# Local attention's softmax in two halves of four heads, one-column routing operations with scalar operands, and a new order of the second stage

## The reference, cut to what matters

```python
def local_attn(x, Wqkv, Wout):            # 8 heads of 64, windows of 64 rows
    q, k, v = map(towin, split(x @ Wqkv.T, 3))
    ke, ve = (expand(k), expand(v))       # window before, own, after: 192 keys
    sim = einsum('bhnid,bhnjd->bhnij', q, ke) * SCALE
    sim = where(valid, sim, -1e9)
    attn = softmax(sim, axis=-1)
    return (attn @ ve) @ Wout.T

def route(x, routing_token, num_tokens):  # for queries 256, for keys 512 of 2048 rows
    s = x @ routing_token
    for _ in range(50):
        a = logk - logsumexp(s + bb)
        bb = -relu(s + a)
    return top_k(exp(s + a + bb), num_tokens)

light = local_attn(_ln(x), Wqkv, Wout_l)
heavy = heavy_attn(x[rows chosen], x[rows chosen], ...)
out = null_q everywhere, heavy where chosen; x + out + light
```

## Time and profile before

| what | value |
|---|---|
| median of 3 runs | 3353.71 us (3351.18 to 3353.83) |
| profiled execution | 3355.9 us, its span 3354.0 us, mean granted clock 0.978 |
| PE busy | 3137.5 us, 94% of the span |
| DVE busy | 2644.0 us, 79% |
| ACT, POOL busy | 1535.5 us, 46%; 1608.7 us, 48% |
| stage 2, DVE, one instruction: sadd, olo, yadd, vadd, xlo | 1216, 689, 683, 676, 678 ns |
| stage 2, DVE: reciprocal of den; routing's na | 203, 266 ns |
| stage 2, ACT: pcopy, softexp, ohi | 588, 1918, 582 ns |
| scores of four heads on PE (8 matmuls); pv of a tile (32) | 1.13 us; 1.97 us |
| weights for stage 3, three DMAs | 2048, 1024 and 1024 KB, landing 9.8, 12.2 and 15.4 us after issue |
| store of y, load of XY, load of XL | 256 KB each, landing 3.6, 3.4 and 3.6 us after issue |

### The profile page before, as it was taken

One profiled execution on the slowest core, in us unless ns is written; L12 is line 12 of the kernel. 1 busy time (PEld: TensorE's weight loads), 2 busy tenths in 40 slices (PEclk: granted clock), 3 DMA queues, 4 the chain that ended last, 5 costly groups with the idle time before them and its releaser, 6 DMA issues.

```text
span 3354.0 us, 52534 instructions
## 1 busy us (share of the span) xinstructions
PE 3137.5 (94%) x20930; PEld 2439.9 (73%) x20930; DVE 2644.0 (79%) x4310; ACT 1535.5 (46%) x2509; POOL 1608.7 (48%) x1043
## 2 busy tenths in 40 slices
PE   7999999999999999999979999998999999968998
PEld 4777777777777777777757777776777777756786
DVE  4788888988999999999947788778877885556453
ACT  1566665656665555545533333332233333324343
POOL 1656555555555665656613444443444444464200
PEclk9999999999999999999989999999999999989999
DMA  4001111010102111110120111111122221132100
GB/s 153 30 28 51 41 38 51 28 57 26 69 26 94 51 41 44 50 48 23 64 79 17 51 51 66 52 51 35 64 80 85 70 85 51 51 117 70 32 14 13
DMA packets 87445, 180.05 MB, mean 54 GB/s; under 512 B 9526, under 2 KB 10294, under 8 KB 85664
## 3 DMA queue, kind: packets, MB, share of 16 engines
q1 hardware_dynamic: 82512, 161.73, 14.0%
q0 software_dynamic: 3968, 10.50, 1.0%
q10 hardware_dynamic: 720, 4.46, 0.3%
HBM read 106.05 MB, written 70.60 MB: 53 GB/s over the span
## 4 chain that ended last, share of the span: by engine, by line
PE 67%; DVE 23%; issue 6%; ACT 2%; POOL 1%; DMA 1%; SPq 1%; POOLq 0%; DVEq 0%; ACTq 0%
PE ps L263 14%; PE ps L265 13%; PE ps L264 13%; PE ps L258 8%; PE ps L270 5%; PE ps L477 4%; PE ps L1125 3%; PE ps L1105 2%; PE ps L486 2%; DVE mx L639 2%; DVE Sb L633 2%; DVE rcol L1267 2%; PE ps L1699 2%; DVE sTa L677 1%; DVE dw L1228 1%
## 5 line engine op out<-in xcount | busy, mean ns | idle before, releaser
L823 POOL TENSOR_TENSOR Sb<-Sb,dn 128x1232 f32<-128x1232 f32 x128 | 294.8, 2303 | 276.8 <-DVE dn L647 276.8
L818 POOL TENSOR_TENSOR Sb<-Sb,mx 128x1232 f32<-128x1232 f32 x128 | 289.1, 2258 | 284.3 <-DVE mx L639 282.1
L1514 POOL TENSOR_TENSOR Sw<-Sw,dw 128x2048 f32<-128x2048 f32 x64 | 230.7, 3604 | 372.4 <-DVE dw L1231 372.4
L773 ACT COPY PT<-ps 77x512 f32<-77x512 f32 x512 | 292.1, 578 | 183.5 <-PE ps L477 182.5
L258 PE MATMUL ps<-KB,QT 128*128 128x308 f32 x1024 | 329.9, 431 | 43.2 <-DVE XB L659 26.8
L1509 POOL TENSOR_TENSOR Sw<-Sw,mw 128x2048 f32<-128x2048 f32 x64 | 232.3, 3629 | 231.4 <-DVE mw L1223 231.4
L1458 ACT COPY PU<-ps 128x512 f32<-128x512 f32 x256 | 139.5, 588 | 405.3 <-PE ps L270 405.3
L477 PE MATMUL ps<-ident,Sb 128*77 128x128 f32 x2048 | 295.2, 277 | 1.7 <-POOL Sb L823 1.3
L477 PEld LDWEIGHTS ps<-ident,Sb 128*77 128x77 f32 x2048 | 242.8, 147 | 71.0 <-issue 33.6
L633 DVE TENSOR_TENSOR Sb<-ps,dlt 128x308 f32<-128x308 f32 x512 | 233.1, 464 | 32.7 <-PE ps L258 30.7
L258 PEld LDWEIGHTS ps<-KB,QT 128*128 128x128 f32 x1024 | 169.0, 191 | 104.1 <-DVE XB L659 44.8
(11 more groups left out here) (275 smaller groups left out, 8148.1 us busy)
## 6 DMA issues: line engine op xcount, KB each, us to landing
XB<-in_x SPq DMA_DIRECT2D x16, 1024.0 KB, 5.3
x_scratch<-XB SPq DMA_DIRECT2D x16, 1024.0 KB, 4.3
XB<-x_scratch SPq DMA_DIRECT2D x16, 1024.0 KB, 5.7
x_scratch<-XB SPq DMA_DIRECT2D x64, 256.0 KB, 2.0
XL<-x_scratch SPq DMA_DIRECT2D x64, 256.0 KB, 3.6
XY<-x_scratch SPq DMA_DIRECT2D x64, 256.0 KB, 3.4
y_scratch<-XY SPq DMA_DIRECT2D x64, 256.0 KB, 3.6
out<-yo SPq DMA_DIRECT2D x64, 256.0 KB
```

Of the source, the lines that this page charges most:

```text
L773: A.copy(PT[:, 4 * g:4 * g + 4, :], ps[0:NK, bank("PT", n, g), :].rearrange("p (c n) -> p c n", c=4)).then_inc(a_pt, 1)
L818: G.tensor_tensor(sv, sv, last(mx[:, n % 2, :], NK), ALU.subtract).then_inc(g_sub, 1)
L823: G.tensor_tensor(sv, sv, last(dn[:, n % 2, :], NK), ALU.mult).then_inc(g_norm, 1)
L1514: G.tensor_tensor(sv, sv, last(dw[:, n % 2, :], 256), ALU.mult).then_inc(bg_norm, 1)
```

## The change

It has three parts. In the routing, three operations on single columns are written as one tensor with scalar operands (`tensor_scalar`) in place of two tensors (`tensor_tensor`, `scalar_tensor_tensor`): `M`, `T` and `dd`. In the local attention, `smax`, `sub`, `softexp`, `den` and `norm` become two instructions per tile, each for four heads (128x1024), with their semaphores counted twice per tile; `ptrans` waits for its own half. All four tables of stage 2 get new places.

```diff
--- before.py
+++ after.py
@@ -142,17 +142,18 @@
 
 
 
-TILE_B = {"loadxy": (18,), "scores": (-5, 20), "sadd": (5, 39), "smax": (56,), "sub": (136,), "softexp": (142,),
-        "den": (115,), "norm": (215,), "ptrans": (151, 156, 171, 174), "pcopy": (184, 186, 197, 205), "pv": (184,),
-        "ohi": (230,), "olo": (204,), "wo": (213,), "yadd": (229,), "yo": (477,), "storey": (270,)}
-BLOCK_B = {"loadxl": (-766, -741, -690, -490), "tail": (-269,), "ln": (-650, -619, -561, -306),
-        "turn": (-319, -317, -299, -296), "xhi": (-294, -289, -266, -260), "xlo": (-298, -297, -294, -293),
-        "qk": (-278, -261, -258, -232, -202, -163, -143, -126),
-        "qkcopy": (-248, -217, -171, -162, -131, -111, -97, -72), "edge": (-53,), "v": (-96, -58, 1, 50, 59),
-        "vadd": (-32, -23, 26, 75, 78)}
-GATHER = {"grows": (-228, -148, -102, -44, -39, 91), "gstats": (82,), "grs": (216,), "gnorm": (127,),
-        "gsq": (505,), "gpow": (679,), "gfin": (1443,)}
-ROUTE = {"rtp": 25, "rtv": 37, "rta": 60, "rts": -102}
+TILE_B = {"loadxy": (-232,), "scores": (-9, 36), "sadd": (15, 41), "smax": (20, 67), "sub": (257, 294),
+        "softexp": (89, 126), "den": (114, 117), "norm": (341, 349), "ptrans": (116, 122, 137, 144),
+        "pcopy": (141, 162, 174, 175), "pv": (183,), "ohi": (220,), "olo": (203,), "wo": (207,), "yadd": (241,),
+        "yo": (537,), "storey": (62,)}
+BLOCK_B = {"loadxl": (-990, -867, -797, -732), "tail": (-130,), "ln": (-600, -519, -517, -324),
+        "turn": (-336, -334, -302, -297), "xhi": (-296, -294, -269, -267), "xlo": (-300, -299, -293, -291),
+        "qk": (-291, -285, -250, -244, -206, -179, -161, -134),
+        "qkcopy": (-231, -221, -186, -181, -160, -134, -90, -81), "edge": (80,), "v": (-105, -46, 3, 46, 59),
+        "vadd": (-48, -20, 39, 73, 106)}
+GATHER = {"grows": (-98, -77, -20, 70, 190, 271), "gstats": (102,), "grs": (424,), "gnorm": (139,),
+        "gsq": (833,), "gpow": (580,), "gfin": (1915,)}
+ROUTE = {"rtp": 21, "rtv": 35, "rta": 55, "rts": -246}
 
 
 def order_b():
@@ -1040,6 +1041,10 @@
 
             return 16 * (e // 17) + min(e % 17, 15)
 
+        def weights(n, p):
+
+            return Sw[:, n % 2, 1024 * p:1024 * p + 1024].rearrange("p (h n) -> p h n", h=4)
+
         def values(i):
             return 5 if i % 4 == 3 else 4
 
@@ -1110,7 +1115,7 @@
 
             def ptrans(n, q):
                 p = take_b("PT", n, q)
-                pe.wait_ge(bg_norm, n + 1)
+                pe.wait_ge(bg_norm, 2 * n + q // 2 + 1)
                 turn4(p, Sw[:, n % 2, 512 * q:512 * q + 512]).then_inc(b_pt, 1)
 
             def pv(n, i):
@@ -1218,17 +1223,16 @@
                                 ps[:, b0:b0 + 2, :].rearrange("p b (k n) -> p (b k) n", k=2),
                                 mid(msk[:, which, :], 4), ALU.add).then_inc(bv_sadd, 1)
 
-            def wmax(n, i):
-                ve.wait_ge(bv_sadd, 2 * n + 2)
-                V.tensor_reduce(mw[:, n % 2, :], Sw[:, n % 2, :].rearrange("p (h n) -> p h n", h=8), X,
-                                ALU.max).then_inc(bv_max, 1)
-
-            def den(n, i):
-                ve.wait_ge(ba_exp, n + 1)
-                V.tensor_reduce(dw[:, n % 2, :], Sw[:, n % 2, :].rearrange("p (h n) -> p h n", h=8), X,
-                                ALU.add).then_inc(v_chain, vc.up())
+            def wmax(n, p):
+                ve.wait_ge(bv_sadd, 2 * n + p + 1)
+                V.tensor_reduce(mw[:, n % 2, 4 * p:4 * p + 4], weights(n, p), X, ALU.max).then_inc(bv_max, 1)
+
+            def den(n, p):
+                d = dw[:, n % 2, 4 * p:4 * p + 4]
+                ve.wait_ge(ba_exp, 2 * n + p + 1)
+                V.tensor_reduce(d, weights(n, p), X, ALU.add).then_inc(v_chain, vc.up())
                 ve.wait_ge(v_chain, vc.n)
-                V.reciprocal(dw[:, n % 2, :], dw[:, n % 2, :]).then_inc(bv_den, 1)
+                V.reciprocal(d, d).then_inc(bv_den, 1)
 
             def olo(n, i):
                 ve.wait_ge(ba_ohi, n + 1)
@@ -1264,7 +1268,7 @@
                     it, part_ = lse(k)
                     if part_ == 0:
                         new_na(it)
-                        V.tensor_tensor(M, smax, na, ALU.min).then_inc(v_chain, vc.up())
+                        V.tensor_scalar(M, smax, na, None, ALU.min).then_inc(v_chain, vc.up())
                         ve.wait_ge(v_chain, vc.n)
                         V.tensor_scalar(zr[:, :], sr[:, :], na, M, ALU.min, ALU.subtract).then_inc(bv_z, 1)
                 elif k == BITS - 2:
@@ -1283,7 +1287,7 @@
                         ve.wait_ge(b_rt, 3 + ITERS - 1 + q)
                         V.tensor_scalar(sel, ps[:, p, 0:1], kcol, None, ALU.is_ge).then_inc(bv_rt, 1)
                         ve.wait_ge(bv_rt, 3 + q)
-                        V.scalar_tensor_tensor(T, dd, sel, T, ALU.mult, ALU.add).then_inc(v_chain, vc.up())
+                        V.tensor_scalar(T, dd, sel, T, ALU.mult, ALU.add).then_inc(v_chain, vc.up())
                     else:
                         ve.wait_ge(ba_e, ITERS)
                     ve.wait_ge(v_chain, vc.n)
@@ -1291,7 +1295,7 @@
                         V.tensor_scalar(cand.bitcast(I32), T.bitcast(I32), 1 << (29 - q), None,
                                         ALU.bitwise_or).then_inc(v_chain, vc.up())
                         ve.wait_ge(v_chain, vc.n)
-                        V.tensor_tensor(dd, cand, T, ALU.subtract)
+                        V.tensor_scalar(dd, cand, T, None, ALU.subtract)
                         V.tensor_scalar(zr[:, :], sr[:, :], cand, 0.0, ALU.is_ge, ALU.add,
                                         accum_out=part).then_inc(bv_z, 1)
                     else:
@@ -1462,9 +1466,9 @@
                 ac.wait_ge(b_wo, n - 1)
                 A.copy(OT[0][:, n % 2, :, :], quad(bank_b("PV", n))).then_inc(ba_ohi, 1)
 
-            def softexp(n, i):
-                ac.wait_ge(bg_sub, n + 1)
-                A.activation(Sw[:, n % 2, :], Sw[:, n % 2, :], ACT.Exp).then_inc(ba_exp, 1)
+            def softexp(n, p):
+                ac.wait_ge(bg_sub, 2 * n + p + 1)
+                A.activation(weights(n, p), weights(n, p), ACT.Exp).then_inc(ba_exp, 1)
 
             def rt(k):
                 if LSE <= k < BITS - 2:
@@ -1503,15 +1507,15 @@
                 if i % 4 == 3:
                     G.memset(KU[:, s, :, 576:640], 0.0).then_inc(bg_edge, 1)
 
-            def sub(n, i):
-                sv = Sw[:, n % 2, :].rearrange("p (h n) -> p h n", h=8)
-                gp.wait_ge(bv_max, n + 1)
-                G.tensor_tensor(sv, sv, last(mw[:, n % 2, :], 256), ALU.subtract).then_inc(bg_sub, 1)
-
-            def norm(n, i):
-                sv = Sw[:, n % 2, :].rearrange("p (h n) -> p h n", h=8)
-                gp.wait_ge(bv_den, n + 1)
-                G.tensor_tensor(sv, sv, last(dw[:, n % 2, :], 256), ALU.mult).then_inc(bg_norm, 1)
+            def sub(n, p):
+                gp.wait_ge(bv_max, 2 * n + p + 1)
+                G.tensor_tensor(weights(n, p), weights(n, p), last(mw[:, n % 2, 4 * p:4 * p + 4], 256),
+                                ALU.subtract).then_inc(bg_sub, 1)
+
+            def norm(n, p):
+                gp.wait_ge(bv_den, 2 * n + p + 1)
+                G.tensor_tensor(weights(n, p), weights(n, p), last(dw[:, n % 2, 4 * p:4 * p + 4], 256),
+                                ALU.mult).then_inc(bg_norm, 1)
 
             def yo_(n, i):
                 gp.wait_ge(bv_y, n + 1)
```

## The result

The changed kernel takes 3261.43 us (median of 4 runs, 3259.53 to 3267.83) against 3353.77 for the kernel before beside it: ratio 0.973, interval 0.9713 to 0.9746, 92 us faster. The profiled execution has a span of 3257.7 us and a clock of 0.987. The forecast was 3299 with a range of 3268 to 3336. The direction was right, the gain was forecast 38 us too small, and the measured time lies outside the range.

The account below looks back on a forecast made before the run. The prediction took stage 2 to be bound by TensorE, with 90 us of holes behind late DVE steps. Gains of 22 (logsumexp rounds), 15 (bits), 3 (indices) and 15 (end), 55 us off 3353.7, gave 3299, range 3268 to 3336.

Parts of the forecast that it names:

- What bounds the kernel: Stage 2: TensorE is the busiest engine with 90 us of holes; only holes and clock lost behind them can be won.
- Rival 3: One-column scalar forms in the routing wait as well; halves leave 5 us and the end 12: 3337 us, chance 0.05.
- The wait moves there: Logsumexp rounds: the DVE row behind M, 345 to 1280 ns before, inherits the wait, now shorter and once less.
- What it buys is latency: Softmax halves: first four heads reach PE earlier, and a POOL instruction holds DVE at most 1.9 us.
- The clock: Behind each PE hole part of the work runs at 1.2 instead of 2.4 GHz, counted as 1.2 us per hole.
- (a): PE order: first-half ptrans moves directly behind wo(n-1); 2 us of slack, so it costs nothing.
- (b): DVE at a block's start: first xlo ends some 8 us after scores, PE needs it after 8.5, so holes close.
- (c): POOL order: yo(n-2) fills the exponential's time; sub(n,1) queues behind edge(i), about 5 us later, at no cost.
- (d): SP queue: loads and stores move up, SP stands still 3.6 us per store; DVE may wait for XL in the index stretch.
- (e): Stage 2's end: gather pairs move between POOL's sub halves; last tiles take 11.3 us each, the end gains 15 (5 to 20).
- Number 2: Rival where everything closes in stage 2: gain 29 + 21 + 12 + 20 = 82 us, 3272 us, chance 0.10.
- The signs: Profile marks: column forms under 300 ns, PE waits under 6 us, clock 0.99, no XY wait, stage 3 55 us earlier.

Follow-up runs that it names:

- e8: Kernel before with the three scalar-operand column operations and the softmax halves together, everything else in the old order; ratio 0.9776 to the kernel before.
- e4: Changed kernel with all four groups of a tile's weight transposes in one row on PE again; 3284.8 us, ratio 0.9791 to the kernel before.
- e1: Kernel before with only the three one-column operations in scalar-operand form; ratio 0.9863 to the kernel before.
- e3: Kernel before with only the softmax steps in halves, each second half directly behind the first, columns and order as before; ratio 0.9808.
- e6: Kernel before with only the changed kernel's order, each softmax step once at its second half's place, columns as before; ratio 1.0625.
- e7: Changed kernel with the DMA-issuing steps on SP (loadxy, storey, loadxl, index steps) back at their old places; ratio 0.9783 to the kernel before.
- e9: Changed kernel with a block's fourth layer norm row behind the first two xlo, and olo ahead of the routing step; ratio 0.9714 to the kernel before.

## Why the prediction was wrong, step by step

**The step that failed** is the price of PE's busy time in the sum. Windows from tile 0 to tile 56 of the kernel before, e8 and after (columns as in the earlier trace rows):

```profile
1764.47:2866.29 1101.82, 1045.41 (x6629) 822.96 (x6630) 871.41 (x1143) 375.02 (x647) 487.81 (x220) 0.98 0.18 58
```

```profile
1765.12:2803.97 1038.85, 1025.15 (x6629) 811.62 (x6630) 757.44 (x1308) 379.97 (x702) 505.48 (x331) 1.00 0.19 62
```

```profile
1763.01:2794.79 1031.78, 1015.84 (x6635) 813.41 (x6636) 760.82 (x1310) 385.42 (x703) 508.18 (x332) 1.00 0.19 64
```

The forecast took 40 us for these tiles (22, 15 and 3); 70.0 came. Of them 40.5 are holes that closed (56.4 to 15.9 us) and 29.6 are a shorter busy time for the same work. The forecast priced that busy time at 1.2 us for each of seven holes and 3.3 us in the bits, 11.7 us at most. It fell by 20.3 us with the old order already (e8), where the clock goes from 0.98 to 1.00, and by another 9.3 us through the new order, which the prediction set at nothing. The holes alone were near the forecast where it looked closely (13.9 us of the 20.3 counted in the rounds, 17.8 of 17.7 in the bits) and above it in the index stretch (6.5, where holes and clock together were put at 3) and from tile 48 to 56 (2.3 for nothing).

**What bounds the kernel** was right as far as it went: a PE stage with holes, DVE late behind POOL. The sentence "only holes and what the clock loses behind them can be won" failed. The 1.6 us of hole in 195 hid a row of transposes that costs 1.7 us a block in the old order and 2.1 in e4, 1.0 of the 1.7 while PE counts as busy.

**Part 1** was right in kind: under 300 ns, waiting for nobody, 200 to 276 ns. The Trainium skill's rule that `tensor_scalar` too can block ("SBUF — State Buffer", section "Who interferes with whom") isn't seen on one column, in the 109 instances of the three; on 128x128 it is (e1: mean 1748 ns). Rival 3 is out. "The wait moves there" was right for columns alone (85.6 us in e1) and wrong beside the halves: L1273 sums to 32.0 us, where before had 32.8.

**Part 2** was right in sizes (1.90 us, 128 times) and wrong in worth. "What it buys is latency" and a bound of 1.9 us on a wait missed that waiting falls by more than half; e3 alone is 64 us, where rival 3 left 5 to the halves outside the end. That is also where the index stretch's gain comes from (9.7 us with halves alone, 1.3 with columns alone). I had it at 3, between a loss on the queue and 12.

**The clock** is the mis-sized term. "I count 1.2 us for each hole" rests on too little: the transposes behind the hole alone give 0.8 (1.97 against 1.14, and the earlier trace rows), the rest was judgement, and the block shows 1.9 to 3.3 for a hole of 3.15 us (before against e8). In tiles 0 to 24 the clock's part is 12.4 us (448.8 to 436.4 us of busy time from before to e8) against the 8.4 counted. That moves my upper bound for the logsumexp rounds from 29 to 33, and the measured 29.7 lies inside. The rest of that term's miss is choice: I took 22 because the holes closed "with half a microsecond to spare". They closed but for 0.8 us a block, and those 0.8 cost no clock. In the bits PE's busy time falls by 4.9 us from before to e8 and by 6.0 to after (160.4 to 154.5, tiles 24 to 32), where I had 3.3.

**Part 3.** (a) "Cost nothing" for the split of `ptrans` missed its gain: the whole order gains 7.0 us on the old one from tile 0 to 56 (e8 against after), and without the split it loses 16.6 (e4). That PE does not wait for `norm` held (0.6 us in two waits from 1762 to 2882); e6 shows what the same order costs without halves. (b) held but for 0.8 us. (c) shows in no wait of PE. (d) feared stalls of SP in the index stretch; none shows in a wait of PE, and DVE's waits for XL there fall from 26.9 us to 5.3. The new places on SP are no gain over the kernel before there either: they avert a loss of 12 us that the old places would bring under the new order (e7), by putting the store ahead of index steps that wait for DVE. The prediction didn't see that need. (e) and the end: 24.8 us against 15 (1.7 of it is stage 3, and 1.7 the last block without routing). The rounds of the last tiles are 11.1 us, forecast 11.3, and the wait for XY is gone. Of the 14.5 us that the order adds to e8 there, e7 loses 11 with the old places on SP. The 5 us that I set against it were not all there: `olo(63)` lost about 1.1 us behind the statistics, and no store behind the 4 MB held `yo` long (0.9 us).

**The rivals.** Number 2, everything closes, was nearest (3272), and it was still short by 11 us, for the clock and the transposes. I gave it 0.10 although step (b) said that the holes of the rounds would close and part 1 that the waiting in the bits ends.

**The signs** named for being right held for the one-column forms, the waits for the bit counts, the clock, the 128 halves and XY. PE's waits for `xlo` are 6.5 us (7.9 with one before a projection) and not under 6, the row behind `M` is no slower, and stage 3 begins 95 us earlier and not 55.

## What to carry to other kernels

Where an engine's work waits behind another engine's long instructions, halve those first: here the waiting fell by more than the length (104 to 43 us), and an order paid that loses 210 us without the halves. Price a hole of TensorE by comparing busy time of a whole block of equal work, not by the first instructions behind it, and look at short waits that recur (0.24 us at each row of transposes in e4 stood for 0.43 us of time). When a step is moved, list each step it passes on its queue, and read the wait at the next stage's start: e9 made tile 63 earlier by 5.5 us, and one unplanned crossing took it back.

## What the runs showed of the hardware

- The same hole of 2.25 us before the same transposes of a block's rows left PE's work at full clock in two blocks of five (1.00) and cost 1.4 and 2.8 us of busy time in the others (0.98 and 0.96); 3.70 us cost 1.5 to 2.5 in each of five, and 0.80 us nothing that could be seen. What decides between the two at 2.25 us stays open.
- TENSOR_SCALAR on 128x1 stays at 200 to 276 ns beside POOL's work; TENSOR_TENSOR on 128x1 went to 3524 ns, and TENSOR_SCALAR on 128x128 has a mean of 1748 ns where POOL's instruction takes 3.6 us (e1) and 626 ns where it takes 1.9 (e8).
- Sixteen transposes into two banks take 2.23 us in a row (from 2752.18 to the next matmul at 2754.41 in e4) and 1.80 us in two parts (0.96 and 0.84, to 2730.99 in after), though the wait that the trace names is only 0.24 us.
